# New orders for the self-attention stage, twelve maxima moved into the convolutions, and a second group's keys built by GpSimd

## What is computed

```python
# layer 0, on group-normalised x
conv_out = conv3x3(x) + conv_b                       # 192 channels
k, q, v  = split(x @ qkv_w + qkv_b)                  # 8 heads of 8
logits   = q @ k.T + rel_w(q) + rel_h(q)             # 1024 x 1024 a head
attn     = softmax(logits) @ v @ attn_w + attn_b     # 64 channels
x        = x + concat(conv_out, attn)
# layer 1, t = x as tokens
u        = layernorm(t)
t        = t + softmax(u W_q (u W_k).T / sqrt(128)) u W_v W_o + b_o + u
u        = layernorm(t)
r        = softmax(mean(u) @ Wr + br); r = softmax(r * scale)
w, e     = top2(r); w = softmax(w)
t        = t + layernorm(sum_k w_k * FFN_{e_k}(u) + u)
```

## Time and profile before

| | us |
|---|---|
| runs of the kernel before | 2072.32, 2077.03, 2077.78 |
| profiled execution, its own time | 2077.25 |
| its span in the trace | 2075.5 |
| TensorE (PE) busy, 10088 matmuls | 1992.4 (96%) |
| VectorE (DVE) busy | 1419.5 (68%) |
| ScalarE (ACT) busy | 1282.0 (62%) |
| GpSimd (POOL) busy | 258.5 (12%) |

### The profile page before, as it was taken

The page is one execution under the profiler, slowest core; times in us unless marked ns, Lnnn a source line. Parts: engine busy times, 40 slices in busy tenths (PEclk is TensorE's granted clock), DMA queues, the critical chain, the costliest instruction groups (busy, mean ns, idle before and its releaser), DMA issues. The chain is left out here.

```text
span 2075.5 us, 27716 instructions
## 1 busy us (share of the span) xinstructions
PE 1992.4 (96%) x10088; PEld 1386.6 (67%) x10088; DVE 1419.5 (68%) x2111; ACT 1282.0 (62%) x2203; POOL 258.5 (12%) x279
## 2 busy tenths in 40 slices
PE   6999999999999999999999998999999969999997
PEld 4888888854545455445545447888888758888886
DVE  7777775677777777777777756777777535566555
ACT  4444543557777777777777766777767545566554
POOL 3000000031222222222223100000000000010000
PEclk9999999899999999999999999999999979999999
DMA  4344557874555554544445321222221163333441
GB/s 120 98 120 159 169 204 223 247 194 93 108 108 107 119 112 108 108 107 108 108 107 138 96 64 58 87 87 87 87 86 52 42 242 145 147 143 142 152 153 51
DMA packets 136791, 253.43 MB, mean 122 GB/s; under 512 B 23376, under 2 KB 87632, under 8 KB 132688
## 3 DMA queue, kind: packets, MB, share of 16 engines
q1 hardware_dynamic: 128848, 226.45, 39.7%
q0 software_dynamic: 7680, 25.17, 3.5%
q10 hardware_dynamic: 128, 0.03, 0.0%
HBM read 143.81 MB, written 107.24 MB: 121 GB/s over the span
## 5 line engine op out<-in xcount | busy, mean ns | idle before, releaser
L881 DVE TENSOR_REDUCE a_nmax<-a_sm 128x1 f32<-128x1024 f32 x512 | 603.6, 1220 | 186.1 <-PE a_sm L901 185.7
L1168 ACT ACTIVATE p_shared<-a_st 128x512 f32<-128x512 f32 x1024 | 557.0, 597 | 237.6 <-PE a_st L1196 236.4
L1211 PE MATMUL a_pv<-p_shared,a_va 128*32 128x512 f32 x2048 | 272.5, 604 | 0.0
L1196 PE MATMUL a_st<-a_qf,a_kf 121*128 121x512 f32 x704 | 252.2, 437 | 4.7 <-PEq L1235 2.5
L1196 PEld LDWEIGHTS a_st<-a_qf,a_kf 121*128 121x128 f32 x704 | 118.8, 188 | 197.1 <-ACT p_shared L1168 186.1
L901 PE MATMUL a_sm<-a_kf,a_qf 120*128 120x512 f32 x704 | 203.7, 407 | 1.8 <-PEq L252 1.8
L2223 DVE SCALAR_TENSOR_TENSOR x_h_lo<-x_hid,x_wts,x_h_hi 128x512 fp32r<-128x512 f32 x128 | 95.8, 750 | 139.7 <-ACT x_h_hi L2184 139.6
L2313 PE MATMUL x_h_ps<-x_v_hi,x_w 128*128 128x512 f32 x512 | 184.1, 401 | 0.0
L2327 PE MATMUL x_y_ps<-x_h_hi,x_w 128*128 128x512 f32 x512 | 181.3, 396 | 0.0
L2180 ACT ACTIVATE x_hid<-x_h_ps,x_bias 128x512 f32<-128x512 f32 x128 | 88.5, 692 | 139.7 <-PE x_h_ps L2313 139.7
L901 PEld LDWEIGHTS a_sm<-a_kf,a_qf 120*128 120x128 f32 x704 | 131.8, 193 | 38.0 <-DVE a_mrow L894 5.6
(11 more groups left out here) (317 smaller groups left out, 3391.1 us busy)
## 6 DMA issues: line engine op xcount, KB each, us to landing
x_w<-w_d SPq DMA_DIRECT2D x31, 1024.0 KB, 8.8
rel_d<-p_shared SPq DMA_DIRECT2D x12, 2048.0 KB, 11.5
a_qf<-rel_d SPq DMA_DIRECT2D x22, 512.0 KB
a_qf<-rel_d SPq DMA_DIRECT2D x44, 256.0 KB
c_xtok<-in_x SPq DMA_DIRECT2D x8, 1024.0 KB, 6.3
va_d<-c_va SPq DMA_DIRECT2D x16, 512.0 KB, 7.0
a_va<-va_d SPq DMA_DIRECT2D x32, 256.0 KB, 15.5
a_w_st<-in_L_ffn_W POOLq DMA_DIRECT2D x32, 256.0 KB, 4.4
```

The lines of the kernel that those rows point to most:

```text
L881: nc.vector.tensor_reduce(nmax[:, h, t:t + 1], sm[k % 2][:], axis=AX.X, op=ALU.max, negate=True).then_inc(sm_read, 1)
L1168: nc.scalar.activation(probs[:, t % 2, h, half * HALF:(half + 1) * HALF], st[half][:], ACT.Exp).then_inc(exp_done, 1)
L1196: nc.tensor.matmul(st[half][:], kf[j][0:ROW_M + 1, h, t * P:(t + 1) * P], qf[j][0:ROW_M + 1, h, 2 * t // TT, half * HALF:(half + 1) * HALF ...
L1211: m = nc.tensor.matmul(pv[32 * h:32 * h + 32, cols], va[j][:, t, h, :], probs[:, t % 2, h, cols], start=t == 0, stop=t == TT - 1, skip_gro ...
```

## The change

- **Maxima**: `PASSES = 12`. In the last image's convolutions, TensorE makes the logits of the first group's tiles 0 to 11 (`first_logits`), two behind each of the units `c0` 0, `c1` 0, `c0` 3, `c1` 3 and one behind each second relative piece, in the two PSUM tiles `c_wide`. VectorE reduces them at the same places. The first waits for the group's queries and keys (`loaded`) and for the last values.
- **Opening block**: it starts at pass 8, with tiles 12 on. `AT` becomes `(3, 12)`, and two warm matmuls go in front of each relative step of the second table. GpSimd, not ScalarE, builds `kf[1]`, at the block's start.
- **Self-attention**: `BETWEEN` is rewritten; `OPENING` replaces it for image 0 and `LAST` for image 7, which takes in what `TAIL` did. In `BETWEEN`, `out` 3 now comes before `probs` 1, `mix` 3 in slot 4 in place of 3, two `grow` steps at the end of slot 0 and the start of slot 1, `out` 1 and two `grow` steps in slot 7. For the last image `out` 3 goes ahead of `turn` 2, and the last two pairs' norm is cut in two steps, `vvar_of` and `vapply_of`.
- **Experts**: the split of the input goes by halves of the tokens instead of halves of the channels and behind the third softmax; the first expert's bias is loaded behind its four weight pieces; GpSimd zeroes a tile (`h_lo`), and TensorE runs 2, 3, 10 and 4 warm matmuls of 128 x 512 around the router's products.

```diff
+    PASSES = 12
...
+        PASS_AFTER = {("c0", 0): (0, 1), ("c1", 0): (2, 3), ("c0", 3): (4, 5), ("c1", 3): (6, 7),
+                      ("rel", 5 * RU + 1): (8,), ("rel", 5 * RU + 3): (9,), ("rel", 5 * RU + 5): (10,), ("rel", 5 * RU + 7): (11,)}
...
+                        if b == B - 1:
+                            for i in PASS_AFTER.get((what, t), ()):
+                                dve.wait_ge(group.sm_done, i + 1)
+                                nc.vector.tensor_reduce(group.nmax[:, i // TT, i % TT:i % TT + 1], wide[i % 2][:], axis=AX.X, op=ALU.max, negate=True
+                                                        ).then_inc(group.sm_read, 1)
...
+                def first_logits(i):
+
+                    h, t = i // TT, i % TT
+                    if i == 0:
+                        pe.wait_ge(group.loaded, 16 * group.LOADS)
+                        pe.wait_ge(va_ready, B + 1)
+                    pe.wait_ge(group.doubled, h + 1)
+                    if i > 1:
+                        pe.wait_ge(group.sm_read, i - 1)
+                    for part in range(2):
+                        m = nc.tensor.matmul(wide[i % 2][:, part * HALF:(part + 1) * HALF], group.queries[0:ROW_M, h, part, t * P:(t + 1) * P],
+                                             group.keys[0:ROW_M, h, part * HALF:(part + 1) * HALF], start=True, stop=True)
+                    m.then_inc(group.sm_done, 1)
...
+                        if b == B - 1:
+                            for i in PASS_AFTER.get((what, t), ()):
+                                first_logits(i)
...
-        passes = [("logits", 0, t) for t in range(AHEAD)] + [("pass", s, None) for s in range(STEPS)]
-        AT, WARM = (4, 14), 4
+        passes = [("pass", s, None) for s in range(group.PASSES - AHEAD, STEPS)]
+        AT, WARM = (3, 12), 4
         order = passes[:2]
         for k, p in enumerate(passes[2:]):
             if k < AT[0]:
                 order += [("warm", k, i) for i in range(WARM)]
-            elif not any(at <= k <= at + RU for at in AT):
+            elif k > AT[1]:
...
                 make_identity(nc, pool, ident[:], made)
+                for h in range(HG):
+                    last = nc.gpsimd.tensor_copy(kf[1][:, h].rearrange("p (a n) -> p a n", a=2), group.both_halves)
+                last.then_inc(built[1], 1)
...
-                    if (what, i, n) == ("rest", 0, RU - 1):
-                        for h in range(HG):
-                            last = nc.scalar.activation(kf[1][:, h].rearrange("p (a n) -> p a n", a=2), group.both_halves, ACT.Copy)
-                        last.then_inc(built[1], 1)
...
         BETWEEN = [
...
-            [("probs", 2, 0), ("mix", 2, 1), ("apply", 0, 1), ("half", 0, 0), ("vapply", 1, -1), ("mix", 3, 1), ("grow", 3, 0)],
-            [("var", 1, 1), ("values", 0, 0), ("ut", 0, 1), ("ut", 1, 1), ("grow", 4, 0), ("probs", 3, 0), ("grow", 5, 0), ("turn", 2, -1)],
...
-        TAIL = [("out", 2), ("probs", 7), ("turn", 0), ("vpair", 2), ("half", 3), ("turn", 1), ("values", 3), ("turn", 2),
-                ("out", 3), ("vpair", 3), ("turn", 3)]
...
+            [("vvar", 1, -1), ("probs", 2, 0), ("apply", 0, 1), ("mix", 2, 1), ("grow", 3, 0), ("half", 0, 0)],
+            [("mix", 3, 1), ("values", 0, 0), ("ut", 0, 1), ("ut", 1, 1), ("probs", 3, 0), ("grow", 4, 0), ("grow", 5, 0)],
...
+        OPENING = [
...
+        LAST = [
...
+             ("vapply_of", 2, 0), ("out", 3, 0), ("turn", 2, 0), ("vvar_of", 3, 0), ("vapply_of", 3, 0), ("turn", 3, 0)]]
...
         def period(b, s, before, after):
 
             steps = []
             for i in range(TT):
                 steps.append(("scores", i, b, s))
-                steps += [(what, k, b + d, s if d == 0 else 1 - s) for what, k, d in BETWEEN[i]
+                steps += [(what, k, b + d, s if d == 0 else 1 - s) for what, k, d in (OPENING if b == 0 else BETWEEN if after else LAST)[i]
...
-            run([(what, k, B - 1, 1) for what, k in TAIL])
...
+                        elif what == "vapply_of":
+                            q = pair(k % 2)
+                            dve.wait_ge(c_done, n * NCS + c_at("turn", k % 2) + 1)
...
-                        sp.dma_start(bias[s][:, k], bias_d[e]).then_inc(small_loaded[s][k], 16)
                         if first and k == 0:
                             for f in range(FC):
                                 sp.dma_start(bits(w[s][:, k, 0:2, :, tile(f)]), w_d[e, :, 0:2, :, tile(f)]).then_inc(first_loaded[f], 16)
-                        else:
+                        sp.dma_start(bias[s][:, k], bias_d[e]).then_inc(small_loaded[s][k], 16)
+                        if not first or k:
...
+                nc.gpsimd.memset(bits(h_lo[HB - 1][:]), 0.0).then_inc(consts, 1)
...
-                            nc.scalar.activation(v_hi[s][:, k], vT[s][:, k], ACT.Copy).then_inc(vhi_ready, 1)
+                            nc.scalar.activation(v_hi[s][:, :, half(k)], vT[s][:, :, half(k)], ACT.Copy).then_inc(vhi_ready, 1)
...
-                run([("split", c, 0, 0) for c in range(KC)])
                 softmax(wrow[:], best[:, 0:TOPK], 2)
...
+                run([("split", j, 0, 0) for j in range(2)])
...
+                def warm(count):
+                    for _ in range(count):
+                        nc.tensor.matmul(y_ps[1][1][:], h_lo[HB - 1][:, 0:P], h_lo[HB - 1][:], start=True, stop=True)
+
+                pe.wait_ge(consts, 1)
+                warm(2)
                 pe.wait_ge(router_loaded, 32)
                 pe.wait_ge(factor_ready, 1)
                 for c in range(KC):
                     m = nc.tensor.matmul(logits, vm[:, c, :], wr[:, c, :], start=c == 0, stop=c == KC - 1)
                 m.then_inc(product_done, 1)
+                warm(3)
                 pe.wait_ge(factor_ready, 2)
 
                 nc.tensor.matmul(loads, ones[:, 0:B], rw[:], start=True, stop=True).then_inc(product_done, 1)
-                pe.wait_ge(consts, 1)
+                warm(10)
+                pe.wait_ge(consts, 2)
                 pe.wait_ge(factor_ready, 3)
                 nc.tensor.matmul(spread, ones[:], diag[:].rearrange("b c k -> b (c k)"), start=True, stop=True).then_inc(product_done, 1)
+                warm(4)
```

More of the change, by code:

```diff
@@ L1667, in self_attention @@
-        TAIL = [("out", 2), ("probs", 7), ("turn", 0), ("vpair", 2), ("half", 3), ("turn", 1), ("values", 3), ("turn", 2),
-                ("out", 3), ("vpair", 3), ("turn", 3)]
+            [("out", 2, -1), ("probs", 7, -1), ("vt", 1, 0), ("turn", 0, -1), ("grow", 0, 0), ("norm", 0, 1), ("grow", 1, 0)],
+            [("norm", 1, 1), ("proj", 0, 1), ("grow", 2, 0), ("half", 3, -1), ("turn", 1, -1), ("probs", 0, 0), ("mix", 0, 1)],
+            [("mix", 1, 1), ("values", 3, -1), ("var", 0, 1), ("proj", 1, 1), ("out", 3, -1), ("probs", 1, 0)],
```

86 lines of the change are left out of this document (47 added, 39 removed).

## The result

| | us |
|---|---|
| kernel before, 18 runs | median 2073.95, 2067.83 to 2079.27 |
| changed kernel, 18 runs | median 2081.71, 2077.72 to 2084.31, and two disturbed runs, 2098.52 and 3247.21 |
| ratio, changed to before | 1.0039, 95% interval 1.0024 to 1.0054 |
| profiled executions, before and changed | 2077.25 and 2078.62, spans 2075.5 and 2076.9 |

The prediction was 2071.8, a gain of 0.25%. The time lies in the stated range of 2060 to 2087, but the change is a loss, clear of its interval. Two things are to be explained: a mechanism, that the early stages lost more than they were to, and a size, that the two traces differ by 1.4 us where the medians differ by 7.8.

The account below looks back on a forecast made before the run. TensorE was taken as the bound, so other engines' edits count only for waits they end. Terms 22.3 - 9.4 + 1.0 - 10.8 - 8.1 - 0.5 = -5.5 from 2077.25 gave 2071.8 us, range 2060 to 2087.

Parts of the forecast that it names:

- convolutions: Last image's convolutions: wait for keys, half clock behind it, added passes, maxima and hand-overs make them longer, +22.3 us.
- opening block: Opening block: second table at full clock and last store issued sooner shorten it from 62.9 to 53.5 us, -9.4.
- first image: Self-attention, image 0: `OPENING` gives its early slots less to do, +1.0 us (0 to +2).
- six middle images: Self-attention: `x` loaded sooner and `mix` 3 behind six score matmuls save 1.8 us an image, -10.8 in six.
- last image and tail: Self-attention's end: `LAST` removes waits on `b_v` and the copies of `turn`, 3.3 us stays, -8.1 (-4 to -9).
- experts with router: Router and experts: bias out of the weights' way by 0.5, zeroing at +0.5, -0.5 us kept (-2 to +0.5).
- The stall: Convolutions, behind `c0` 0: TensorE waits for keys queued behind the relative stores on SyncE's queue, +10.6 us.
- Rival 2: Convolutions: keys land early at 354.8, stall is 3.4 us and the clock does not fall, 2062.1 us; chance 0.10.
- Maxima 8 to 11: Last stretch of the convolutions, among the relative pieces: four maxima add 4 x 1.22 us on VectorE, +4.9.
- Why the clock should stay full: Opening block: the clock fell behind ScalarE's building of the keys; with that removed, the second table saves 9.7 us.
- rival 3: Opening block: the half clock comes again in the second table, +9.7 us, 2081.5; chance 0.10.
- Rival 1: Middle images: ScalarE becomes the wait, an image loses 1.5 us instead of gaining 1.8, 2091.6 us; chance 0.13.

Follow-up runs that it names:

- experiment 5: The kernel before, unchanged, run once more for another profiled execution: 2069.28 us.
- experiment 4: The kernel before with one edit: GpSimd, not ScalarE, builds the second group's keys at the opening block's start. 2069.85 us, ratio 0.9982.
- experiment 3: The changed kernel with the first group's keys loaded ahead of the relative stores on SyncE's queue: 2071.21 us, ratio 0.9992 to the kernel before.
- Experiments 8 and 9: The kernel of experiment 3 with 8 and with 4 maxima in the convolutions instead of 12: 2066.91 us (ratio 0.9960) and 2061.16 us (0.9939).
- experiment 10: Convolutions of before, late stages as changed, second group's keys built on GpSimd, plus opening block's tables earlier (`AT, WARM = (1, 10), 4`): 2059.72 us, ratio 0.9941.
- experiment 7: Convolutions of before, late stages as changed, keys built on GpSimd, but `mix` 3 back in slot 3 of the middle images: 2066.66 us, 7.7 more.
- experiment 14: The changed kernel, unchanged, run once more for a further profiled execution: 2080.12 us.
- experiment 11: The 8-maxima kernel of Experiments 8 and 9 with both tables at the opening block's start (`AT, WARM = (0, 9), 4`): 2072.84 us, ratio 1.0000.

## Why the prediction was wrong

Two steps failed. A saving of 9.7 us was taken from a half clock that about half of the runs of before don't have. And the four maxima among the relative pieces were counted as 4.9 us of VectorE's time, where the stretch got 9.4 us longer, most of it TensorE's own time at half clock and a wait. By the prediction's own steps, with the first two traces:

| step | predicted | measured |
|---|---|---|
| convolutions | +22.3 | +25.0 |
| opening block | -9.4 | -7.9 |
| main attention | 0 | +0.2 |
| first image | +1.0 | -0.6 |
| six middle images | -10.8 | -8.8 |
| last image and tail | -8.1 | -6.7 |
| experts with router | -0.5 | +0.2 |
| sum | -5.5 | +1.4 |

**The baseline.** From the predicted change of -5.5 to the measured one of +7.8 it is 13.3 us. Of these, 6.9 lie in the steps of the table, 3.3 in the trace of before, which is that much above its median of 2073.95, and 3.1 in the trace of the changed kernel, that much below its own. The second part was there to be asked about. The sum is made against 2077.25, "the median is 2077.03, 0.2 below"; three runs were shown, 2072.32, 2077.03 and 2077.78, and the prediction took the middle one as the kernel's time, where the trace was of the slow way. "The second table runs at the full clock, which saves 7 steps x 1.39 = 9.7" is a saving that about half of the runs of before had already (experiment 5: 2069.28 with the break and without the half clock). Against the median of before it is worth 4 to 5 us, and experiment 4 measured that. Against the trace of experiment 5, which goes the fast way, the opening block of the changed kernel is 0.7 us shorter (55.4 for 56.1), and the change costs 9.4 us of span: +26.0 up to the main attention, -16.6 behind it.

**The stall.** Foreseen and right: 11.2 us for 10.6, from SyncE's queue, and experiment 3 shows the cause. Rival 2, keys that overtake the stores, which the Trainium skill ("DMA: Bandwidth & Descriptors", Queues, rings and completion order) leaves possible, did not happen in any of four traces (11.2, 11.2, 10.3 and 11.5 us).

**The relative pieces.** The step that failed is "Maxima 8 to 11 ... add 4 x 1.22: +4.9". The stretch from the end of `c1` 3 to the end of the convolutions took 18.7 us instead of 9.3, where the prediction has 4.9 more and 0.9 for passes 6 and 7. It was counted as VectorE's time alone. What was missed is that the two maxima ahead of the first piece stop TensorE for 1.7 us, and that the clock falls behind this broken stretch. At half clock TensorE's own eight matmuls set the step, 1.7 instead of 0.9 us; TensorE is then busy 4.00 of 4 us, and VectorE waits for it, through ScalarE, for up to 1.0 us a piece. The maxima between the pieces hide in these waits: what is paid there is the half clock and the logits' own matmuls, not VectorE's 1.22 us. Experiments 8 and 9 bear this out: with 8 maxima, none of them between the pieces, the step is 1.7 as well, and with 4 there is neither the wait nor the half clock. That the wait brings the clock down is the order of events in every trace with it, and no run has the one without the other. The 3.7 for the passes were about right; the half clock behind the stall cost less than the 2.5 put down for it, some 1.6 (the unit and the four logits matmuls behind the stall took 5.4 us, and 3.8 at full clock in the kernel with 4 maxima).

**The opening block.** "The block ends with whichever is last" held for the store, 41.4 + 12.8 us, where 39.1 + 12.5 were predicted. But the block then hardly depends on the number of maxima: with all of them in it, store and VectorE end together (experiment 4), so fewer maxima leave the end where the store puts it, and TensorE then stands idle for 14.05 us before the main attention. The table by stage, of the block alone, in the changed kernel and in experiments 5, 9 (4 maxima) and 10, shows what the prediction did not ask about:

```profile
395.70:451.10 55.40, 40.87 (x224) 33.57 (x224) 30.57 (x27) 25.19 (x33) 12.25 (x14) 0.87 0.96 300
```

```profile
369.10:425.20 56.10, 50.56 (x258) 38.92 (x259) 43.64 (x39) 27.93 (x37) 8.43 (x9) 0.96 0.95 296
```

```profile
374.90:429.90 55.00, 49.11 (x256) 38.70 (x256) 39.66 (x35) 25.20 (x33) 12.28 (x14) 0.97 0.97 302
```

```profile
370.10:425.30 55.20, 51.00 (x252) 38.58 (x252) 44.06 (x39) 24.18 (x33) 12.22 (x14) 0.95 0.96 301
```

VectorE's work differs by 13 us, the block by one, and the 16 DMA engines are busy 0.95 to 0.97 of it. Share times length is 53.0 to 54.3 us in all eleven traces of the block that were compared, the slow way of before included. So the transfers leave a block of about 54 us (an estimate from these shares) little to gain, whatever is moved out; no run has changed the transfers, so this is argued, not shown. Experiments 8 and 9 show the other side: where the maxima went, each costs about a microsecond. On its terms the change was a loss in the early stages from the start; the prediction had that (+12.9), and the sum was saved only by the late ones.

**Why the clock should stay full.** The explanation, that the break on ScalarE's building was enough of a cause, fell with experiment 5: the same 2.49 of 4 us with the clock full behind it. The table did run at full clock in the changed kernel, but that may be luck: the reason is not shown. The rule of the Trainium skill ("TensorE: Matmul & The Clock Gate", HAM oscillation), that breaks without work are the cause, fits the stall (half clock behind 11.2 us without work) but not the relative pieces: there the clock fell at 383 behind waits of which the longest is 1.7 us, with TensorE busy 2.33 of 4 us. That is the mechanism of rival 3, in another place, and the measurement decides.

**Middle images.** The mechanism was half right. "`out` 3 goes ahead of `probs` 1, so `x` is loaded sooner" was wrong: the load is issued 16.3 us into the image (1433.22 in that beginning at 1416.97) where it was 16.4 (1419.24 in that at 1402.83). "`mix` 3 goes behind six score matmuls" was right and is all of it (experiment 7). The term was 1.8 an image and measured 1.5, which is the idle time that went (1.7 to 0.2 an image): the extra 0.5 for a restart behind a wait was not there. The "2.4 us" of cover was misread too: score matmuls last 0.4 but start 0.23 apart, so six are 1.4 us, just enough for a wait of 1.5. Rival 1, ScalarE as the wait, did not come.

**First image, last image, experts.** The first image was to lose 1.0 and won 0.6: the wait for the exponentials fell from 3.3 to 1.1 us, and a wait of 3.2 for the attention's output came; in experiment 14 it was 2.0 us longer, so this term is not settled. The last image's mechanism was right, -6.7 for -8.1. Idle time fell from 11.4 to 5.9 us, where 3.3 were to stay: the last norm's wait is 2.3, but 1.1 for `out` 3 stayed as before, and 1.0 of the 3.3 for the copies of `turn`. In the experts the first product came 1.0 us later behind the zeroing, where 0.5 was put down, and the weights were issued 0.6 later with it, so that the 0.5 of the bias did not come.

## What to carry over

Moving work off an engine pays only in the block that this engine ends: look for what ends last in the block that is relieved, its transfers included (their share times its length is a guess at how short it can get), and for the queue that feeds the block that is loaded, since a new consumer turns a transfer's place in the queue into a stall. If the few runs shown do not agree, ask which of them the trace is, and take no saving from a stretch that another run may not have.

## What was not expected of the hardware

The same program, with the same break in TensorE's work (2.49 of 4 us busy), has its next 20 us now at 1.2 and now at 2.4 GHz, in a block that takes 64 or 56 us. The clock stayed down for 20 us of a busy TensorE in the trace of before, and from about 373 to 405 in experiment 11, whereas behind the 11 us stall it came back within 4 us of work. And an earlier store need not land earlier: issued 35.4 us into the block in experiment 10 it took up to 18.4 us to land, issued 39.3 us into it in experiment 4 up to 14.8, so that the last part landed 54.2 and 54.5 us into the block.
